# Layer 2 of a four-layer kernel: half of its softmax by subtraction on VectorE, its ffn three steps nearer to the attention, and the ffn's first weights loaded in layer 1

## The reference

```python
# attention: 32 heads of 16 features, 8 key/value heads, keys and values from the context
q = (query @ Wq).reshape(b, sq, 32, 16).transpose(0, 2, 1, 3)
k = jnp.repeat(k, 4, axis=1); v = jnp.repeat(v, 4, axis=1)
scores = jnp.einsum('bhqd,bhkd->bhqk', q, k) * 16 ** (-0.5)
out = jnp.einsum('bhqk,bhkd->bhqd', jax.nn.softmax(scores, axis=-1), v)
x = x + out.transpose(0, 2, 1, 3).reshape(b, sq, 512) @ Wo
# ffn: 64 experts of rank 16, the best 16 of each row weighted by a softmax
top_vals, top_idx = jax.lax.top_k(xf @ Wr.T, 16)
G = zeros.at[rows, top_idx].set(softmax(top_vals))
x = x + 2 * jnp.einsum('nkr,kdr->nd', jnp.einsum('nd,krd->nkr', xf, A) * G[:, :, None], B)
```

## Time and profile before

| | us |
|---|---|
| median of 3 runs | 1694.81 |
| lowest and highest run | 1686.79, 1695.62 |
| the profiled execution: its time | 1690.08 |
| the profiled execution: its span | 1687.9 |

### The profile page before, as it was taken

The page is one execution under the profiler, slowest core; times in us unless marked ns, Lnnn a source line. Parts: engine busy times, 40 slices in busy tenths (PEclk is TensorE's granted clock), DMA queues, the critical chain, the costliest instruction groups (busy, mean ns, idle before and its releaser), DMA issues. The chain is left out here.

```text
span 1687.9 us, 26011 instructions
## 1 busy us (share of the span) xinstructions
PE 1579.3 (94%) x9516; PEld 1288.2 (76%) x9522; DVE 802.8 (48%) x1633; ACT 780.1 (46%) x2689; POOL 517.0 (31%) x648
## 2 busy tenths in 40 slices
PE   6999988789999999999999999868999999899998
PEld 5877766678888888888888888646545668787876
DVE  4556656354444454554444437743554222242454
ACT  3445443445454544545454565456553112454551
POOL 5666664132222222222222224332321000124323
PEclk9999999999999999999999999979999999999999
DMA  8000000102010010101010100003000001311101
GB/s 235 15 7 8 7 1 13 51 1 94 26 38 26 15 39 12 38 26 39 26 38 26 38 1 1 26 1 140 1 1 13 12 5 49 109 50 30 43 21 57
DMA packets 42942, 58.22 MB, mean 34 GB/s; under 512 B 26064, under 2 KB 33616, under 8 KB 39872
## 3 DMA queue, kind: packets, MB, share of 16 engines
q1 hardware_dynamic: 41136, 56.05, 10.5%
q10 hardware_dynamic: 1616, 0.51, 0.1%
q0 software_dynamic: 64, 0.00, 0.0%
HBM read 48.94 MB, written 2.10 MB: 30 GB/s over the span
## 5 line engine op out<-in xcount | busy, mean ns | idle before, releaser
L1684 ACT ACTIVATE big<-pb 128x128 f32<-128x128 f32 x384 | 106.5, 277 | 310.6 <-PE pb L785 203.0
L2068 POOL TENSOR_TENSOR big<-big 128x512 f32<-128x512 f32 x96 | 99.9, 1040 | 271.5 <-DVE big L1368 271.1
L1735 ACT ACTIVATE big<-pb,big 128x128 f32<-128x128 f32 x384 | 135.8, 367 | 69.1 <-issue 43.6
L800 PE MATMUL pb<-wkh,CXh 128*128 128x256 f32 x512 | 149.5, 292 | 1.6 <-DVE big L1353 1.6
L1363 DVE TENSOR_REDUCE big<-pb 128x4 f32<-128x512 f32 x96 | 65.9, 686 | 175.0 <-PE pb L824 167.4
L800 PE MATMUL pb<-wkl,CXh 128*128 128x256 f32 x512 | 144.3, 282 | 0.0
L800 PE MATMUL pb<-wkh,CXl 128*128 128x256 f32 x512 | 143.6, 281 | 0.0
L2058 POOL TENSOR_SCALAR big<-big 128x6 f32<-128x6 f32 x64 | 13.0, 203 | 424.5 <-ACT big L1684 423.9
L1158 DVE TENSOR_TENSOR X<-X,pb 128x512 f32<-128x512 f32 x128 | 86.8, 678 | 71.7 <-PE pb L1006 29.5
L849 PE MATMUL pb<-woh,oh 128*128 128x512 f32 x256 | 113.1, 442 | 3.0 <-DVE wol L1184 2.9
L785 PE MATMUL pb<-wqh,CXh 128*128 128x512 f32 x256 | 103.1, 403 | 10.6 <-DVE wql L1184 5.1
(11 more groups left out here) (253 smaller groups left out, 3924.9 us busy)
## 6 DMA issues: line engine op xcount, KB each, us to landing
big<-in_w SPq DMA_DIRECT2D x17, 1024.0 KB, 4.9
big<-in_w SPq DMA_DIRECT2D x8, 768.0 KB, 5.5
big<-in_w SPq DMA_DIRECT2D x8, 512.0 KB, 3.6
o<-o SPq DMA_DIRECT2D x96, 32.0 KB, 1.9
X<-in_x SPq DMA_DIRECT2D x8, 256.0 KB, 5.5
big<-in_cn SPq DMA_DIRECT2D x8, 256.0 KB, 2.7
CXlf<-in_cT SPq DMA_DIRECT2D x8, 256.0 KB, 5.5
big<-in_wa SPq DMA_DIRECT2D x1, 2048.0 KB, 8.0
```

What stands on the lines that cost most here:

```text
L800: a = pe.matmul(bank(p)[:, s * 256:s * 256 + 256], kv_rows(x, c, 2 * t + s), y[:, 256 * c:256 * c + 256], start=(n == 0), stop=(n == 11), ...
L1684: y = a.activation(sq[i % 2], bank(p)[:, j * width:j * width + 128], ACT.Square, accum_out=ss[i % 2][:, first + j:first + j + 1])
L1735: y = a.activation(e_[:, c], bank(p)[:, c], ACT.Exp, bias=m[j % 2][:, k:k + 1], scale=1.0, accum_out=z[j % 2][:, k:k + 1])
L2068: g.tensor_tensor(quarters(e_), quarters(e_), bc(r[j % 2], 128), MUL).then_inc(*on.to(S.pn))
```

## The change

- `l2_e`: row pair 0 of a batch is no longer eight exps with a bias. VectorE subtracts the maxima (an addition of the negated ones, from PSUM, into the SBUF tile `sm`) in `l2_s`, after both maxima, and ScalarE does one exp over 512 columns in place. Row pair 1 is as before.
- `l2_a`'s two copies and `l2_v`'s copy go from ScalarE to VectorE.
- The order of a step is written out by hand (`batch_steps`: stage, steps late, units), with `l2_z` one step later than before, first in its step, and with `ffn1` as a stage of it, behind `l2_s`. The ffn's stages are nearer to l2_c: f2_rows and f2_turn one step behind it, f2_a and f2_h together two steps behind, f2_b three, f2_o and l3_stats five, l3_rows and l3_turn six. `l2_q` 0 now comes behind a step of `ffn1` and behind `f1_turn` 6. The layer 3 keys and values come in steps 0 to 5 of what is left instead of 0 to 8.
- `f1_turn` from tile 6, `f1_mm` from tile 5 and `l2_turn` from tile 4 use the ring `sh`.
- wa is loaded behind km at the end of layer 1's seventh head, after layer 1's ffn weights have been quantised; wr in `l2_begin`; wb in `f2_begin`, which no longer waits for l2_turn; w3kv in a new stage `l3_load` three steps later. For this wa lies 512 columns further left (wr4 gets 8 columns of padding behind it).

```diff
+    def batch_steps(n, stages):
+        for step in range(n + max(late for _, late, _ in stages)):
+            yield [(name, on(step - late)) for name, late, on in stages
+                   if 0 <= step - late < n and on(step - late) is not None]
...
-    pipe2 = pipeline(range(16), [("l2_q", queries_at)] + [(s, every) for s in l2[1:6]] + [("l2_c", odd)]
-                     + [(s, odd) for s in f2], ("l2_z",))
...
+    pipe2 = batch_steps(16, [("l2_z", 3, every), ("f2_rows", 7, odd), ("l3_rows", 12, odd), ("f2_o", 11, odd),
+                             ("l3_stats", 11, odd), ("f2_b", 9, odd), ("l2_c", 6, odd), ("f2_stats", 6, odd),
+                             ("l2_v", 5, every), ("l2_t", 4, every), ("l2_s", 2, every), ("ffn1", 0, every),
+                             ("l2_a", 1, every), ("l2_e", 2, every), ("l2_q", 0, queries_at), ("f2_a", 8, odd),
+                             ("f2_h", 8, odd), ("f2_turn", 7, odd), ("l3_turn", 12, odd)])
+    kv = {0: [("l3_keys", 0)], 1: [("l3_values", b) for b in range(4)], 2: [("l3_keys", 1)],
+          3: [("l3_values", b) for b in range(4, 8)], 4: [("l3_keys", 2)], 5: [("l3_values", b) for b in range(8, 12)]}
...
-            together(stages, (ffn1, 0), (l2_kv, 0), (pipe2, 9), (ffn1, 9))
+            together(stages, (ffn1, 0), (l2_kv, 0), (ffn1, 9))
     order.append(("l2_begin", 0))
-    for _ in range(8):
-        got = next(pipe2)
-        together(got, (ffn1, min(3, len([s for s in got if s[0] != "l2_e"]))))
-    order.append(("f2_begin", 0))
-    run(16 + 6 - 9, pipe2)
+    for step in range(16 + 6):
+        for name, i in next(pipe2):
+            if name == "ffn1":
+                run(1, ffn1)
+            else:
+                order.append((name, i))
+        if step == 7:
+            order.append(("f2_begin", 0))
+        if step == 10:
+            order.append(("l3_load", 0))
...
+    sh = (0, 5, 6, 7)
     if stage == "f1_turn":
-        return [("p", (3,))]
+        return [("p", (3,) if i < 6 else sh)]
     if stage == "f1_mm":
-        return [("p", (7 if i < 5 else 4,))]
+        return [("p", (7,) if i < 5 else sh)]
     if stage == "l2_turn":
-        return [("p", (2 if i < 4 else 3,))]
+        return [("p", (2,) if i < 4 else sh)]
...
+            def l2_a(b):
...
+                    y = v.tensor_copy(view(VX[b % 5][r], 16 * k, [[32, 4], [1, 16]]),
+                                      view(bank(p)[r], 16 * k, [[32, 4], [1, 16]]))
...
             def l2_s(b):
...
+                on.wait_ge(p0.full, p0.n + 1)
+                on.mark(v.tensor_reduce(m2[2 * b % 4], b0, AX, MAX, negate=True))
+                first = on.n
+                on.wait_ge(p1.full, p1.n + 1)
+                v.tensor_reduce(m2[(2 * b + 1) % 4], b1, AX, MAX, negate=True).then_inc(S.m2, 1)
+                if b >= 3:
+                    turned = PSUM["l2_t", b - 3, 0]
+                    on.wait_ge(turned.full, turned.n + 1)
+                on.wait_ge(S.dve, first)
+                v.tensor_tensor(sm[2 * b % 6].rearrange("p (g k) -> p g k", g=8), b0, bc(m2[2 * b % 4], 64),
+                                ADD).then_inc(p0.free, 1)
...
+            def l2_v(b):
...
+                v.tensor_copy(O2[t % 2].rearrange("p (r b q) -> p r b q", r=4, b=2)[:, :, b % 2, :],
+                              bank(p)[:, 0:256].rearrange("p (r q) -> p r q", r=4)).then_inc(p.free, 1)
...
             def l2_e(b):
-                for rp in range(2):
-                    n, p = 2 * b + rp, PSUM["l2_s", b, rp]
...
+                p0, p1, k0, k1 = PSUM["l2_s", b, 0], PSUM["l2_s", b, 1], 2 * b, 2 * b + 1
+                on.wait_ge(p0.free, p0.n + 1)
+                a.activation(sm[k0 % 6], sm[k0 % 6], ACT.Exp).then_inc(S.e2, 1)
...
+                on.wait_ge(S.m2, b + 1)
+                for k in range(8):
+                    c = slice(64 * k, 64 * k + 64)
+                    y = a.activation(sm[k1 % 6][:, c], bank(p1)[:, c], ACT.Exp, bias=m2[k1 % 4][:, k:k + 1], scale=1.0)
+                y.then_inc(p1.free, 1)
...
                     load(km, d["km"], D.mk)
+                    on.wait_ge(S.mx4, 4)
+                    load(wa, d["wa"], D.f2)
...
             def l2_begin(_):
                 on.wait_ge(l1_done.full, l1_done.n + 1)
                 load(w2o, d["w2o"], D.w2o)
+                load(wr, d["wr"], D.f2)
 
             def f2_begin(_):
-                lt2, x, q = PSUM["l2_turn", 7, "p"], PSUM["f1_mm", 7, "p"], PSUM["l2_q", 3, 3]
+                x = PSUM["f1_mm", 7, "p"]
                 on.wait_ge(x.free, x.n + 1)
-                on.wait_ge(lt2.free, lt2.n + 1)
-                load(wr, d["wr"], D.f2)
-                load(wa, d["wa"], D.f2)
                 load(wb, d["wb"], D.wb)
+
+            def l3_load(_):
+                q = PSUM["l2_q", 3, 3]
                 on.wait_ge(q.full, q.n + 1)
                 load(w3kv, d["w3kv"], D.x3)
```

More of the change, by code:

```diff
@@ L549, in build_program @@
         wr = quarters(carve(R0 + 18528, R0 + 18784)(256))
-        al = carve(RF + 520, RW)
+        al = carve(RF + 8, RW)
         wa = quarters(al(4096))
@@ L1414, in l2_z @@
                     n = 2 * b + rp
-                    e = PSUM["l2_s", b, rp]
-                    on.wait_ge(e.free, e.n + 1)
+                    e = PSUM["l2_s", b, 1]
+                    if rp == 0:
+                        on.wait_ge(S.e2, b + 1)
+                    else:
+                        on.wait_ge(e.free, e.n + 1)
                     on.mark(v.tensor_reduce(z2[n % 2], sm[n % 6].rearrange("p (g k) -> p g k", g=8), AX, ADD))
@@ L1420, in l2_z @@
                     v.reciprocal(r2[n % 2], z2[n % 2]).then_inc(S.r2, 1)
+            def l2_v(b):
+                p, t = PSUM["l2_v", b, "p"], b // 2
+                on.wait_ge(p.full, p.n + 1)
+                if t >= 2:
+                    c = PSUM["l2_c", t - 2, "p"]
+                    on.wait_ge(c.full, c.n + 1)
+                v.tensor_copy(O2[t % 2].rearrange("p (r b q) -> p r b q", r=4, b=2)[:, :, b % 2, :],
+                              bank(p)[:, 0:256].rearrange("p (r q) -> p r q", r=4)).then_inc(p.free, 1)
             def l2_c(t):
@@ L1523, in vector_program @@
                       l1_b=l1_b, l1_s=l1_s, l1_z=l1_z, l1_v=l1_v, l1_d=l1_d, f1_quant=f1_quant,
-                      f1_mm=f1_mm, l2_s=l2_s, l2_z=l2_z, l2_c=l2_c, f2_a=f2_a, f2_h=f2_h,
+                      f1_mm=f1_mm, l2_a=l2_a, l2_s=l2_s, l2_z=l2_z, l2_v=l2_v, l2_c=l2_c, f2_a=f2_a, f2_h=f2_h,
                       f2_o=f2_o, l3_begin=l3_begin, l3_keys=l3_keys, l3_values=l3_values, l3_main=l3_main, l3_q=l3_q, l3_a=l3_a, l3_z=l3_z, l3_v=l3_v, l3_c=l3_c, f3_mm=f3_mm)
@@ L1805, in l2_q @@
                                  scale=0.25).then_inc(p.free, 1)
[L1807 to L1812, removed]
[L1813 to L1831 removed]
+            def l2_e(b):
+                p0, p1, k0, k1 = PSUM["l2_s", b, 0], PSUM["l2_s", b, 1], 2 * b, 2 * b + 1
+                on.wait_ge(p0.free, p0.n + 1)
+                a.activation(sm[k0 % 6], sm[k0 % 6], ACT.Exp).then_inc(S.e2, 1)
+                if b >= 3:
+                    turned = PSUM["l2_t", b - 3, 1]
+                    on.wait_ge(turned.full, turned.n + 1)
+                on.wait_ge(S.m2, b + 1)
[3 more added lines that the diff above has]
+                y.then_inc(p1.free, 1)
             def l2_t(b):
@@ L1841, in l2_t @@
                            bank(p).rearrange("p (x j n) -> p j x n", x=2, j=2)).then_inc(p.free, 1)
-            def l2_v(b):
-                p, t = PSUM["l2_v", b, "p"], b // 2
-                on.wait_ge(p.full, p.n + 1)
-                if t >= 2:
-                    c = PSUM["l2_c", t - 2, "p"]
-                    on.wait_ge(c.full, c.n + 1)
-                a.copy(O2[t % 2].rearrange("p (r b q) -> p r b q", r=4, b=2)[:, :, b % 2, :],
-                       bank(p)[:, 0:256].rearrange("p (r q) -> p r q", r=4)).then_inc(p.free, 1)
             def f2_a(t):
@@ L1937, in scalar_program @@
                       l1_b=l1_b, l1_s=l1_s, l1_t=l1_t, l1_v=l1_v, l1_d=l1_d, f1_turn=f1_turn, l2_kv=l2_kv,
-                      l2_q=l2_q, l2_a=l2_a, l2_e=l2_e, l2_t=l2_t, l2_v=l2_v, f2_a=f2_a, f2_b=f2_b, l3_begin=l3_begin, l3_keys=l3_keys, l3_main=l3_main, l3_q=l3_q,
+                      l2_q=l2_q, l2_e=l2_e, l2_t=l2_t, f2_a=f2_a, f2_b=f2_b, l3_begin=l3_begin, l3_keys=l3_keys, l3_main=l3_main, l3_q=l3_q,
                       l3_e=l3_e, l3_t=l3_t, l3_v=l3_v, l3_c=l3_c)
```

55 lines of the change are left out of this document (19 added, 36 removed).

## The result

The changed kernel takes 1685.23 us (median of 20 runs, 1681.11 to 1689.52); the kernel before, run beside it, takes 1692.41 (20 runs, 1686.14 to 1697.86). The ratio is 0.9963, with a 95% interval of 0.995 to 0.9976: faster by 6.3 us, between 4.1 and 8.5. It is the ratio of the means, 1685.36 and 1691.66; the medians lie 7.2 apart.

What follows compares the result with a forecast made beforehand. TensorE, 94% busy, was taken as the bound, with losses in its waits and low clock after layer 1. Gains of 3.0 (ramp), 6.0 (dense part) and 0 (weights) make 9.0 us off 1694.8: 1685.8 us, range 1676 to 1699.

Steps and rivals of the forecast that it cites:

- ramp: From the end of layer 1 to the end of the second f2_h; 3.0 us to be gained.
- rest: Everything behind the second f2_h; 6.0 us to be gained in the dense part.
- start: Start of layer 2: f1_turn.6 waits for tile 6's quantising in front of l2_q.0; TensorE idle 6.3 us.
- steps 5, 6 and 8: Bare batches of the ramp: loop 4.9 us between scores, work 2.6, 2.3, 2.4; TensorE idle 2.2, 2.7, 2.5.
- Step 2: Ramp: scores.0 wait 0.5 us for the last query copy; then TensorE idles 3.5 until the exps are out.
- Step 3: Ramp: f1_turn.7 waits for tile 7's quantiser with l2_q.1 queued behind it; TensorE idle 1.3 us.
- Part 1: Layer 2's halved exps: ScalarE saves about 1.0 us per batch, bare loop grows from 5.2 to 5.9–6.2; split wins nothing.
- Part 3: Dense part: the 3.4 us gap at layer 3's turns, its 1.6 low clock and 1.0 before last f2_o go; gain 6.0.
- Part 4: Early weight loads (wa, wr, wb, w3kv): TensorE's waits show no DMA, so value 0.
- A: Rival: low clock leaves the ramp and tile 7's quantising slips under l2_q.0; gain 17 us, 1678; chance 0.22.
- B: Rival: short idles between the ramp's bare batches keep TensorE at low clock, some 10 us lost; 1696; chance 0.17.
- C: Rival: VectorE bounds the ramp, a bare batch needs 7.5 us instead of 6.1; 1704; chance 0.08.

Runs made afterwards that it cites:

- keys ahead: The changed kernel with l2_a, holding GpSimd's masked keys, put before layer 1's ffn step (ffn1): 1681.1 us, ratio 0.9941 to the kernel before.
- won by the banks: The kernel before with only the new bank rings for late f1_turn, f1_mm and l2_turn: 1686.43 us, ratio 0.9975.
- the difference above: Ramp of the changed kernel with ffn and layer 3 stages placed as before (131.1 us), less that of the kernel before with new banks alone (126.0): 5.1.
- the query and the keys ahead: The changed kernel with l2_a before ffn1, l2_q.0 before step 1, and l3_rows before l3_keys: 1672.63 us, ratio 0.9906 to the kernel before.
- the first experiment: The changed kernel with row pair 0 back to eight exps on ScalarE, no subtract: 1684.01 us, ratio 0.9954 to the kernel before.
- its ffn as far as before: The changed kernel with layer 2's ffn and layer 3's keys and values exactly where they were before: 1691.2 us, ratio 1.0016 to the kernel before.
- quantiser ahead: The changed kernel with ffn1 before l2_s, so VectorE quantises tile 7 earlier: 1683.44 us, ratio 0.9957 to the kernel before.

## Why the prediction was right, and where not

**The total.** Forecast 1685.8, measured 1685.2. That the two meet to 0.6 us is in part luck: the forecast stood on a median of 1694.8 from three runs, which twenty runs put at 1692.4, and its gain of 9.0 is too large for the 6.3 measured (4.1 to 8.5). Against their own profiled executions, ramp and rest gained 4.4, and 1.4 more fell in front of layer 1's end, which the change does not explain and which also varies between kernels with the same code there. The mechanism held in its main lines (banks and the end of layer 2 win, arithmetic and loads don't), and both terms of the sum were too large: the ramp's by 1.0, the rest's by 1.0 to 3.6. Of the signs that it named for being wrong, the ramp of 115.2 stayed under 118, but the dense part has a gap of its own (1.45 us at 1371.56).

**The ramp, 3.0 forecast, 2.0 measured** (133.3 - 16.1 - 115.2). The walk's idle, step by step:

| step | forecast | measured |
|---|---|---|
| start | 6.3 | 0.94 + 1.12 + 3.47 = 5.5 |
| 2 and 3 | 0.5 + 3.5 + 1.3 | 0.52 + 7.82 = 8.3 |
| 5, 6, 8 | 2.2, 2.7, 2.5 | 1.69, 2.66, 2.08 |
| 10 | 0.8 | 0.78 |
| sum | 19.8 + 0.5 | 21.0 |

The sum is right to 1 us by errors that partly cancel: the start 0.8 and steps 5, 6 and 8 together 1.0 less than forecast, steps 2 and 3 3.0 more. Where it failed is "Step 2" and "Step 3": I queued tile 7's quantiser on VectorE and followed TensorE and ScalarE, but not GpSimd, on which the keys of the next batch stand behind that tile's bias. The step cost 3 us more than the walk had, and keys ahead took 3.8 out of the ramp. The walk followed three queues of four. The same queue also ends the gap of step 6: 2.66 us, released by GpSimd, where the kernel with the keys ahead waits 2.04 for the exps. The bare batches came out near the forecast: these three rows of the timeline of ScalarE after are 5.6 and 6.0 apart (forecast 6.0 to 6.3), and the exp of 512 columns takes 0.63 (0.65), the subtract 0.68 (0.69). Without GpSimd's wait a bare batch takes 5.5 us from scores to scores (1125.90 to 1131.40, and 1150.74 to 1156.24), less than the 5.9 to 6.2 of Part 1.

```profile
1128.99 0.63 ACT L1853 ACTIVATE big<-big 128x512 f32<-128x512 f32 x1 [1.63 <-DVE big L1440]
...
1134.56 0.63 ACT L1853 ACTIVATE big<-big 128x512 f32<-128x512 f32 x1 [0.82 <-DVE big L1440]
...
1140.57 0.63 ACT L1853 ACTIVATE big<-big 128x512 f32<-128x512 f32 x1 [2.06 <-DVE big L1440]
```

Low clock: with the prediction's estimate of 9.5 for before, the same work at the full clock is 133.3 - 20.8 - 9.5 - 16.1 = 86.9, so an estimate of 115.2 - 21.1 - 86.9 = 7.2 is lost to it after, forecast 7.0. The 9.61 of l2_q.0 is 2.5 above the 7.07 of the earlier trace rows, forecast 2.0.

**What the small net hides.** The ramp's 2 us is 7.3 won by the banks and 5.1 given back, by the difference above, by the new order at its start. The prediction saw both sides, idle of 6.3 where l2_q.0 no longer covers tile 6, and 9.7 of bank waits gone, but netted them in one walk and never said that they are separable. Had I written them as two terms, the first could have been kept and the second dropped: with the query and the keys ahead the ramp is 11.0 us shorter.

**Reasons that were wrong.** Part 1 says that "what wins is that l2_z moves a batch later", and the text on the change has it so too. It doesn't: written out, both orders have l2_z of a batch first in the step behind its l2_s, and l2_v, l2_t, l2_s and l2_a in the same order behind it. What changed around them is the place of layer 1's last ffn stages, before the scores in most steps and behind them now, and of l2_q.0. No number of the sum hung on it. And Part 1's longer loop does not show, as the first experiment has it: 5.2 us was the loop of a ScalarE with nothing else to do.

**The rest, 6.0 forecast, 2.4 measured in one pair of traces** (468.5 + 16.1 - 482.2), 5.1 against the kernel with its ffn as far as before, and 5.0 over all traces of either kind. The gaps went as forecast: none at layer 3's first turn, none before the last f2_o. What Part 3 missed is the new 1.45 us twice. It asked what stands in front of the turn on TensorE ("7.9 us of work before their bank is wanted") and not what stands in front of the rows on ScalarE, now that layer 3's keys come just before the rows and the turn just behind. It is the error of step 2 again, on another engine.

**Part 4** held: no worth of the early wa shows, and the ramp is the same to 0.0 without it.

**The rivals.** A (more is won) needed tile 7's quantiser to slip in under l2_q.0; it stood behind the scores, as argued, and the change didn't do it. Where the quantiser was put ahead, the ramp became 3.3 shorter, near the 3 us of idle that A gave it. B (the low clock takes it back) did not happen: bare batches left gaps of 1.69, 2.66 and 2.08 us, and the eight score matmuls behind the first two took 1.13, at the full clock; only those behind the third took 1.90. By the rule that I cited from the Trainium skill, page "TensorE: Matmul & The Clock Gate", section "A second HAM failure mode: psum-queue depth-cycling", B was the likelier case; the trace does not agree for the gaps of 1.69 and 2.66, and does for that of 2.08. C (VectorE bound, a bare batch of 7.5) did not happen: it was 5.5 to 6.1.

## What to carry to other kernels

Where engines run one written order, walk each moved stage through every engine's queue, GpSimd's too: here 4.6 us of a wait of 7.8 went when an instruction that needed nothing no longer stood behind one that waited, and 2 x 1.45 us in the same way. When a change moves the time little, try its parts alone: this one held 7 us of gain and, by difference, 5 us of loss in one stretch, and with three stages moved back or ahead the 6 us became some 16. A wait that is taken away shows the one that lay behind it, so price the new wait before you book the old.

## What the runs showed of the hardware

For one kind of group, how long TensorE had stood still told which clock it got at short and at long gaps, and not between. Groups of eight score matmuls in the timeline after, behind gaps of 1.69, 2.66 and 2.08 us:

```profile
1131.40 1.13 PE L937 MATMUL pb<-big,CXlf 64*128 64x256 f32 x8 [1.69 <-ACT big L1860]
...
1137.48 1.13 PE L937 MATMUL pb<-big,CXlf 64*128 64x256 f32 x8 [2.66 <-POOL big L2114]
...
1156.24 1.90 PE L937 MATMUL pb<-big,CXlf 64*128 64x256 f32 x8 [2.08 <-ACT big L1860]
```

The longer gap of 2.66 was followed by the full clock (1.13), the shorter of 2.08 by a group mostly at the lower (1.90, near the 2.08 of the earlier trace rows). Over the fourteen traces of this case, from 1060 to 1420 us, 66 such groups stand behind a gap. The 24 behind gaps of up to 2.00 us all took 1.13 or 1.14, and the 15 behind gaps of 2.96 us and more all took 2.08. Of the 27 between 2.04 and 2.67 us, 16 took 1.13 or 1.14 and 11 took 1.27 to 1.93. What decides there was not tried.

A small step of VectorE depends on what GpSimd does beside it. Timeline after, the same step of tiles 6 and 7, and GpSimd's memset that runs beside the first:

```profile
1088.10 0.68 DVE L1201 TENSOR_SCALAR big<-big 128x16 f32<-128x16 f32 x1
...
1107.43 0.17 DVE L1201 TENSOR_SCALAR big<-big 128x16 f32<-128x16 f32 x1
```

```profile
1087.85 0.91 POOL L2103 MEMSET big<- 128x640 f32 x1
```

0.68 against 0.17 us, with GpSimd idle in the second case. The step ends 0.02 us after the memset. With the quantiser ahead, the step of tile 7 falls beside GpSimd's masked keys instead (timelines of VectorE and GpSimd):

```profile
1102.84 0.58 DVE L1201 TENSOR_SCALAR big<-big 128x16 f32<-128x16 f32 x1
```

```profile
1102.60 0.79 POOL L2114 TENSOR_TENSOR big<-big 128x256 f32<-128x256 f32 x1 [0.17 <-POOL ve L1988]
```

Here the step takes 0.58 us and again ends just behind GpSimd, and the keys take 0.79 where they take 0.61 in the rows above. In the fourteen traces this step stands 56 times from 1060 to 1120 us: the 15 beside a GpSimd instruction take 0.58 or 0.68, the 41 others 0.17. So it goes with what GpSimd does at that time; no run was made that moves GpSimd's instruction alone.
